# Moving the last two additions of an int8 layer from VectorE to GpSimd, at the end of a four-layer transformer kernel

## What is computed

```python
def _L3_ffn_ref(inp, qweight_t, wscale, bias):
    x = inp.reshape(Bb * Ss, Kk)
    amax = jnp.max(jnp.abs(x), axis=1, keepdims=True)
    iscale = amax / QMAX
    q = jnp.clip(jnp.round(x / jnp.maximum(iscale, 1e-12)), -QMAX, QMAX).astype(jnp.int8)
    d = jnp.matmul(q, qweight_t, preferred_element_type=jnp.int32)
    out = d.astype(jnp.float32) * iscale * wscale[None, :] + bias[None, :]
    return out.reshape(Bb, Ss, -1)
...
x = x + _L3_ffn_ref(_L3_cond_ref(x, itok_B_0_7, ...), ...)
```

## Time and profile before

| | us |
|---|---|
| median of three executions | 3198.6 (3192.68 to 3199.76) |
| the profiled execution, its own time | 3195.55 |
| its span, first to last instruction | 3193.8 |
| busy in it: PE, DVE, ACT, POOL | 3024.6, 1552.8, 1284.7, 1490.8 |
| mean granted TensorE clock | 0.981 |

### The profile page before, as it was taken

How to read it: one execution, slowest core, us unless ns; L and a number is a source line. 1 busy time by engine, 2 the same in 40 slices (tenths; PEclk the granted TensorE clock), 3 DMA queues, 4 the chain that set the end, 5 groups by cost and what they waited for, 6 DMA issues and landing times. The chain is left out here.

```text
span 3193.8 us, 55792 instructions
## 1 busy us (share of the span) xinstructions
PE 3024.6 (95%) x15256; PEld 2022.0 (63%) x15264; DVE 1552.8 (49%) x3979; ACT 1284.7 (40%) x3014; POOL 1490.8 (47%) x1275
## 2 busy tenths in 40 slices
PE   3789999999999999999999999999999996999897
PEld 2466666666666666666666666666666674655554
DVE  5544444444444444444444444444444453656665
ACT  1344444444444444444444444444444441222222
POOL 7355555555555555555555555555555540000000
PEclk9899999999999999999999999999999998999998
DMA  8544444444444344545444444434444454211210
GB/s 291 203 115 122 121 121 121 121 119 120 118 118 118 118 118 118 198 119 169 122 119 119 119 119 119 119 119 119 119 119 119 119 150 164 49 40 31 49 30 13
DMA packets 416154, 377.54 MB, mean 118 GB/s; under 512 B 83427, under 2 KB 347763, under 8 KB 414996
## 3 DMA queue, kind: packets, MB, share of 16 engines
q1 hardware_dynamic: 358484, 186.81, 20.7%
q0 software_dynamic: 50480, 174.40, 17.5%
q10 hardware_dynamic: 7056, 14.46, 1.2%
HBM read 341.23 MB, written 25.85 MB: 115 GB/s over the span
## 5 line engine op out<-in xcount | busy, mean ns | idle before, releaser
L533 DVE CUSTOM_DVE_ANT_0 ps_s<-ps_s,mask 128x544 f32<-128x544 f32 x512 | 375.0, 733 | 940.6 <-PE ps_s L360 781.2
L262 POOL DMA_INDIRECT v_sb<-in_v_rows_w,v_row x504 | 489.7, 972 | 473.9 <-PE ps_oT L385 264.2
L319 PE MATMUL ps_t<-wqkv,xT 128*128 128x512 f32 x1488 | 701.6, 594 | 0.0
L383 PEld LDWEIGHTS ps_oT<-pT,v_sb 128*128 128x128 f32 x4096 | 528.4, 192 | 188.9 <-issue 188.2
L433 ACT ACTIVATE ps_s<-ps_s,nmax 128x544 f32<-128x544 f32 x512 | 352.3, 688 | 586.3 <-DVE nmax L533 519.9
L383 PE MATMUL ps_oT<-pT,v_sb 128*128 128x128 f32 x4096 | 543.1, 276 | 11.6 <-issue 11.5
L343 PE MATMUL ps_t<-wo,oT 128*128 128x512 f32 x1024 | 524.7, 596 | 2.5 <-ACT oT L448 0.9
L359 PE MATMUL ps_s<-k_sb,qT 128*128 128x416 f32 x1024 | 448.0, 519 | 11.4 <-issue 5.7
L448 ACT ACTIVATE oT<-ps_oT 128x128 f32<-128x128 f32 x512 | 142.7, 279 | 685.9 <-PE ps_oT L385 656.4
L543 DVE TENSOR_SCALAR p_sb<-ps_s,rinv 128x544 f32<-128x544 f32 x512 | 401.4, 784 | 23.8 <-DVE rinv L540 0.3
L368 PEld LDWEIGHTS ps_pT<-ident_sb,p_sb 128*128 128x128 f32 x2048 | 251.7, 141 | 187.4 <-issue 181.6
(11 more groups left out here) (219 smaller groups left out, 3545.5 us busy)
## 6 DMA issues: line engine op xcount, KB each, us to landing
k_sb<-in_kT SPq DMA_DIRECT2D x2048, 64.0 KB
v_sb<-in_v_rows_w,v_row POOLq DMA_INDIRECT x512
v_new<-v_raw SPq DMA_DIRECT2D x128, 64.0 KB, 1.9
wo<-in_wo_w POOLq DMA_DIRECT2D x2, 4096.0 KB, 15.2
y_scratch<-y_sb SPq DMA_DIRECT2D x32, 256.0 KB
xT<-x1T_scratch POOLq DMA_DIRECT2D x31, 256.0 KB
tab<-rope_scratch POOLq DMA_DIRECT2D x31, 256.0 KB
wqkv<-in_wqkv_w ACTq DMA_DIRECT2D x6, 1024.0 KB, 10.5
```

The lines of the kernel that those rows point to most:

```text
L262: e.indirect_dma_start(out=v_sb[:, b % 2, c, :], out_offset=None, in_=A["v_rows_w"], in_offset=bass.IndirectOffsetOnAxis(ap=v_row[:, b, c: ...
L319: m = e.matmul(ps_t[bank_of(t)][:, :], xT[:, k, :], wqkv[:, k, 512 * t:512 * t + 512], start=k == 0, stop=k == KC - 1)
L383: e.matmul(ps_oT[:, :], v_sb[:, b % 2, c, h * D:(h + 1) * D], pT[:, u % 2, c, :], start=c == 0, stop=False)
L533: e.tensor_tensor_reduce(out=scores(u), in0=scores(u), in1=mask[:, b % 2, :], scale=-SCALE, scalar=3e38, op0=ALU.add, op1=ALU.min, accum_o ...
```

## The change

GpSimd gets a program for the last stage that runs `output` for every step and half. VectorE no longer runs it. Because GpSimd now reads `x3` and `qf` at its own pace, VectorE waits for `out_ready` of the step before where it next writes `x3` (in `third`) and before it next uses `qf` (in `quantise`).

```diff
+        @block.gpsimd
+        def _(e):
+            def output(k, p):
+                e.wait_ge(event["d_scaled"], 2 * k + p + 1)
+                e.tensor_tensor(qf[p][:, :], qf[p][:, :], bias3[:, :], ALU.add).then_inc(event["d_biased"], 1)
+                e.wait_ge(event["d_biased"], 2 * k + p + 1)
+                e.wait_ge(stored[p], 16 * (k + 1))
+                e.tensor_tensor(outb[p][:, :], qf[p][:, :], x3[p][:, :], ALU.add).then_inc(event["out_ready"], 1)
+            with e.Fori(0, I_STEPS) as k:
+                for p in both:
+                    output(k, p)
...
             def third(k):
                 for p in both:
                     e.wait_ge(event["x3_done"], 2 * k + p + 1)
+                    if not (isinstance(k, int) and k == 0):
+                        e.wait_ge(event["out_ready"], 2 * (k - 1) + p + 1)
...
             def quantise(k, p):
                 e.wait_ge(event["c3_copied"], 2 * k + p + 1)
+                if not (isinstance(k, int) and k == 0):
+                    e.wait_ge(event["out_ready"], 2 * (k - 1) + p + 1)
...
-            def output(k, p):
-                e.wait_ge(event["d_scaled"], 2 * k + p + 1)
-                e.tensor_tensor(qf[p][:, :], qf[p][:, :], bias3[:, :], ALU.add).then_inc(event["d_biased"], 1)
-                e.wait_ge(event["d_biased"], 2 * k + p + 1)
-                e.wait_ge(stored[p], 16 * (k + 1))
-                e.tensor_tensor(outb[p][:, :], qf[p][:, :], x3[p][:, :], ALU.add).then_inc(event["out_ready"], 1)
...
                 rescale(k, 0)
                 if more:
                     mask_states(k + 1, 1)
-                output(k, 0)
                 rescale(k, 1)
-                output(k, 1)
```

## The result

| | before | after |
|---|---|---|
| median of the runs on one chip, us | 3191.11 (3183.74 to 3199.76, 12 runs) | 3206.9 (3198.39 to 3214.99, 12 runs) |
| the profiled execution, us | 3195.55 | 3203.25 |
| its span, us | 3193.8 | 3201.4 |
| ratio, 95% interval | | 1.0048 [1.0032, 1.0063] |

The three executions of before that the prediction knew are among the twelve. The changed kernel is slower by about 0.5%.

A forecast was written before the change was run, and what follows sets the result against it. It took the last stage to be bound by TensorE, busy 91 us of 100, and its waits for VectorE at the joints. Adding 0.4 us at seven joints and 1.4 at the end to 3197.2 gave 3199 us, range 3189 to 3207.

The forecast's parts named there:

- The joint: Between steps, GpSimd's additions hold up VectorE's split, giving back the saving: +0.06 us a joint, 0.4 us for seven.
- The clock: After TensorE's wait at five of seven joints the granted clock drops, costing 1.34 us each; all five drops stay.
- Rival 1: At the joints, no hold-up in the split: -9.4 us, up to -6.7 more from clock drops, 3189 to 3182; chance 0.18.
- The end: Behind the last rescale, the final additions take 2.82 us on GpSimd in place of 1.45: +1.4 us.
- The new waits: VectorE's waits before writing x3 and in quantise, GpSimd's wait for the earlier store, and SP's store: cost nothing.
- The sum of the parts I costed: Whole kernel: 0.4 us at the joints plus 1.4 us at the kernel's end, +1.8 us.
- Taken away: At each joint, without both half 1 additions VectorE's split begins 1.34 us earlier if nothing holds it up; half 0's give nothing.
- The base: Whole kernel: starting time of 3197.2 us, to which the forecast change of 1.8 us and the rivals are added.
- rival 2: In the split at the joint, L1429 is held too: +0.47 us a joint, +7.4 in all, 3204.5 us; chance 0.14.

The follow-up runs named there:

- experiment 1: Changed kernel with seven idle increments on VectorE ahead of its loop, putting the loop's start back at 835: 3188.13 us, ratio 1.0001 [0.9989, 1.0013] against the kernel before.
- experiments 5 to 7: Changed kernel, loop at 835: GpSimd adding 8 of 512 columns, 0.9948; its half-1 additions after split, 0.9972; kernel before reordered, all on VectorE, three ways: 0.9944, 0.9913, 0.9899.
- experiment 6: Changed kernel with its loop at 835, GpSimd's additions of half 1 waiting until half 1's split is done: 3179.45 us, ratio 0.9972 against the kernel before.

## Why the prediction was right and wrong

The range held the time, 3206.9 at its upper end of 3207, but for a cause that it did not have in it. That is luck. The outcome is slower by over 0.2%, to which I gave 0.14, and that chance stood for another mechanism.

**The joint.** Forecast: L1430 0.65, L1431 1.3, TensorE's wait 2.9 to 3.1. Measured: 0.64 to 0.65, 1.26 and 2.87 to 2.88 at all seven joints. Rows 7 to 9 were the right ones to read, and L1429, like L533, passed. The term was +0.06 us and came out at -0.07: GpSimd starts 0.08 us behind the rescale and not 0.20. Its start was taken from the earlier trace rows, where it had waited long for another kind of instruction.

**The clock.** I kept five drops, of 1.34 us each. The kernel of experiment 1 has five, with waits of 2.87 to 2.89 us. The changed kernel has them at four joints, and one more behind VectorE's second pause at 3031, where TensorE had waited 1.88 us. Why the clock falls at some joints and not at others, with waits that are equal to 0.03 us, stays open. Rival 1 said that the drops may go with a wait of 1.6 us. In experiments 5 to 7, with waits of 1.49 us and less at the joints, the granted clock is 1.00 all the way from 2724 to 3116 us. So a drop costs what I took, and no joint with a wait of 1.5 us or less has one. (The prediction counts seven starts in the chain of before. There is an eighth, at 3157.93, with an interval of 59.23; five drops at seven joints is right even so, the fifth being at 3139.)

**The end.** Forecast +1.4, measured +1.2; the hand-over from VectorE was 0.12 us too long, and that between the two additions was right with 0.08. The addition takes 1.26 us, where the earlier trace rows have 1.27, and not the 1.35 that I worked out from the Trainium skill's ratio (GPSIMD Engine Reference, Elementwise — side-by-side cycle accounting): the row was the better guide.

**The new waits.** Costed at nothing. Experiment 1 has them all and is at 1.0001 [0.9989, 1.0013]: right.

**The sum of the parts I costed** was +1.8 us, and experiment 1 measures it: the ratio of 1.0001 is +0.3 us, with an interval from -3.5 to +4.1. By the rows it is 7 x -0.07 + 1.2 = +0.7. The mechanism is shown by the joint, and the sum is not contradicted.

**The failed step** is "Taken away". There I counted the removed instructions only by their time on the path, 1.34 us a joint. That VectorE's program gets shorter, and its loop moves to another place in the code, was costed at nothing by not being named. It is worth 4.0 us at each of four jumps back, 16.1 us in the profiled execution. The other three intervals of the chain were 3.0 us shorter than before (177.3 in place of 180.3), since two of them lost the drop of the clock that they had. Between the ratios of the changed kernel and of experiment 1 lie 0.47%, 15 us. The trace of before shows only 10 packets of instructions in the stage, so its loop's code was held over the jumps; no row told that this hangs on where the loop lies, or what it costs to lose it. By the runs the loop is free of stalls with its head at 832, 835, 851 and 883, and the kernel before stood at 835, three instructions from the edge; counting the instructions ahead of the loop would have told that six fewer are a risk, though not on which side of an edge.

**The base.** I took 3197.2 from three runs and one profile. The twelve runs later gave 3191.11, so the base was 6 us too high, and this hid part of the miss: from the later base the forecast would have been 3193, 14 us below the 3207 measured.

**Rivals.** Rival 1 (no hold-up) and rival 2 (L1429 held too) are both excluded by the joint's rows. Rival 2's sum of +7.4 lies between forecast and result, and has nothing to do with it.

## What to carry to other kernels

Where a change takes instructions out of an engine's program, or puts some in, ahead of or inside a loop of about 256 instructions, look just behind the jump back at that engine's idle time with no releaser, or with one that had long been done, and at the packets of the instruction queue; then measure the change once more with a few idle increments ahead of the loop before judging it. Work is not off an engine's path when it goes to another that holds it up meanwhile: find the place where the first engine waits anyway, and put it there, in its own program. Here that was worth 0.56%, and 0.9% with the split ahead of the rescale, where the move was worth nothing.

## What was not expected of the hardware

- One instruction more or less ahead of a loop of 259 made some 18 us of 3190 (831 against 832: ratios 1.0047 and 0.9991). The pauses are 3.3 to 4.1 and then 1.8 to 2.2 us with the head at 829, one of 5.3 to 5.7 us at 831 and 959.
- In the whole run that queue moved 39 packets before and 59 after: five more for each jump back.
- A custom instruction with two SBUF operands is held up too, 1.58 us in place of 0.51, and GpSimd's addition beside it took 1.43 in place of 1.26. Both sides pay there (experiment 6).
- GpSimd began 0.08 us behind the VectorE instruction that released it, where the earlier trace rows have 0.20.
